# A gated cross-attention and routed-expert layer on one core: the order of four instruction queues between attention and the expert blocks

## The reference

```python
x = x + tanh(g_xattn) * xattn(layernorm(x), ctx)     # 4 x 256 tokens of 256, 64 context rows, 16 heads of 128
h = layernorm(x)                                      # 1024 tokens
combine = top-2 of softmax(h @ gate_w.T), 4 experts   # weight per token and expert, others zero
y = sum_e combine[:, e] * swiglu(h, w1[e], w3[e], w2[e]) + swiglu(h, sw1, sw3, sw2)
x = x + tanh(g_ffn) * y
```

## Time and profile before

| | us |
|---|---|
| median of three runs | 271.18 (270.52 to 271.84) |
| profiled execution | 273.08 |
| its span, first to last instruction | 271.3 |
| TensorE busy | 227.8 (84%) |
| VectorE / GpSimd / ScalarE busy | 148.1 / 131.2 / 119.1 |
| mean granted TensorE clock | 0.957 |

### The profile page before, as it was taken

The page is one execution under the profiler, slowest core; times in us unless marked ns, Lnnn a source line. Parts: engine busy times, 40 slices in busy tenths (PEclk is TensorE's granted clock), DMA queues, the critical chain, the costliest instruction groups (busy, mean ns, idle before and its releaser), DMA issues.

```text
span 271.3 us, 4800 instructions
## 1 busy us (share of the span) xinstructions
PE 227.8 (84%) x1490; PEld 194.0 (72%) x1490; DVE 148.1 (55%) x352; ACT 119.1 (44%) x225; POOL 131.2 (48%) x121
## 2 busy tenths in 40 slices
PE   3999999989969769757776688989999999998920
PEld 1786777879968659646565567878988889887820
DVE  1399889998848556455636417663433435333210
ACT  3376787386543543454423323334344433433310
POOL 4134311748958567844525552164446465452422
PEclk9999999999999995799999959999999999999995
DMA  7753553121413412420002310032423424332131
GB/s 214 228 150 143 164 185 120 58 58 58 138 24 113 138 33 103 135 80 19 19 22 67 108 54 7 0 60 41 77 39 45 75 41 59 58 50 30 23 39 21
DMA packets 12775, 20.99 MB, mean 77 GB/s; under 512 B 2032, under 2 KB 7664, under 8 KB 12752
## 3 DMA queue, kind: packets, MB, share of 16 engines
q1 hardware_dynamic: 9104, 15.71, 18.4%
q0 software_dynamic: 3648, 4.98, 11.5%
HBM read 16.10 MB, written 4.59 MB: 76 GB/s over the span
## 4 chain that ended last, share of the span: by engine, by line
PE 41%; DMA 23%; issue 10%; ACT 8%; POOL 7%; DVE 7%; POOLq 1%; DVEq 1%; SPq 1%; ACTq 0%
DMA out_dram<-probs,tok 19%; PE bankR L358 5%; PE bankQ L242 4%; PE bankQ L244 4%; PE bankQ L243 4%; PE bankP L242 4%; PE bankP L243 4%; PE bankP L244 4%; POOL reg L1411 3%; DMA raw<-kvq_dram 3%; ACT reg L762 2%; ACT probs L805 2%; POOL rstd L1400 2%; PE bankP L335 2%; DMA probs<-x2d,tok 1%
## 5 line engine op out<-in xcount | busy, mean ns | idle before, releaser
L1438 POOL DMA_INDIRECT out_dram<-probs,tok x19 | 30.1, 1587 | 53.3 <-ACT probs L805 30.6
L1411 POOL TENSOR_TENSOR reg<-raw,reg 128x768 fp32r<-128x768 f32 x16 | 29.3, 1833 | 16.5 <-ACT reg L762 16.5
L242 PE MATMUL bankS<-reg,hT 128*128 x76 | 22.9, 301 | 2.4 <-DVE hT L1200 1.5
L1429 POOL DMA_INDIRECT probs<-x2d,tok x19 | 20.2, 1065 | 5.6 <-issue 5.1
L1379 POOL TENSOR_TENSOR w_lo<-raw,w_hi 128x512 fp32r<-128x512 f32 x8 | 10.4, 1301 | 24.4 <-ACT w_hi L686 24.4
L244 PE MATMUL bankS<-reg,hT 128*128 x76 | 21.4, 281 | 0.0
L243 PE MATMUL bankS<-reg,hT 128*128 x76 | 21.4, 281 | 0.0
L1005 DVE TENSOR_TENSOR PT_lo<-bankR,PT_hi 128x512 fp32r<-128x512 f32 x16 | 10.8, 680 | 18.3 <-ACT PT_hi L734 18.3
L792 ACT CAST hT<-bankR 128x512 fp32r<-128x512 f32 x19 | 11.1, 586 | 20.5 <-PE bankR L550 20.5
L1200 DVE TENSOR_TENSOR hT<-bankR,hT 128x512 fp32r<-128x512 f32 x19 | 13.1, 691 | 10.1 <-ACT hT L792 10.1
L1392 POOL TENSOR_TENSOR probs<-probs,rcp 128x1024 f32<-128x1024 f32 x8 | 15.3, 1910 | 4.3 <-DVE rcp L989 4.3
(11 more groups left out here) (232 smaller groups left out, 727.2 us busy)
## 6 DMA issues: line engine op xcount, KB each, us to landing
raw<-ffn_dram SPq DMA_DIRECT2D x18, 384.0 KB, 3.6
raw<-kvq_dram SPq DMA_DIRECT2D x7, 384.0 KB, 3.3
probs<-wo_dram SPq DMA_DIRECT2D x8, 256.0 KB, 2.7
x_sb<-x_dram SPq DMA_DIRECT2D x1, 1024.0 KB, 6.0
x2d<-xn SPq DMA_DIRECT2D x8, 128.0 KB, 1.7
out_dram<-x_sb SPq DMA_DIRECT2D x8, 128.0 KB, 1.7
probs<-x2d,tok POOLq DMA_INDIRECT x19, 2.9
out_dram<-probs,tok POOLq DMA_INDIRECT x19, 3.8
```

The costliest lines, as they stand in the source:

```text
L242: eng.matmul(acc, l_hi, r_hi, start=start, stop=False, **kw)
L1411: pool.tensor_tensor(lo, raw[:, (m + 2) % RS, :], hi.bitcast(F32), ALU.subtract).then_inc(wf_lo, 1)
L1429: pool.indirect_dma_start(out=x_blk[:, i % 4, :], out_offset=None, in_=x2d[:, :], in_offset=bass.IndirectOffsetOnAxis(ap=tok[:, i:i + 1], ...
L1438: pool.indirect_dma_start(out=out[:, :], out_offset=bass.IndirectOffsetOnAxis(ap=tok[:, i:i + 1], axis=0), in_=y_blk[:, i % 4, :], in_offs ...
```

## The change

No computation is added or removed; queues are put in another order, with two waits moved and two added.

- GpSimd subtracts weight tiles two behind the tiles that ScalarE rounds in the same iteration.
- VectorE reads the logits ahead of its part of `split_p`, and chooses the experts of group 0 ahead of the fifth tile's logits; the block list comes earlier, `spots`, the token copies and `settle(1)` are placed anew.
- TensorE makes the first shared up product ahead of the last half of attention; `turn_x2(7)` and the logits come later.
- ScalarE evicts the shared tile n-3 ahead of the activation of tile n.
- The last shared down product and its eviction stand inside block 0.
- GpSimd gathers block n-3 ahead of the addition of shared tile n, and the first gather waits for the first four stored tiles only.

```diff
@@ TensorE
                 wait(pe, h_gate, i - 1)
+                if i == 0:
+                    pe.wait_ge(s_gate, NT)
...
             places(0)
+            pe.wait_ge(wf_lo, JS)
+            pe.wait_ge(x1_ok, NT - 2)
+            shared_up(0)
             attend(7, 1)
             turn_x2(6)
-            pe.wait_ge(wf_lo, JS)
             pe.wait_ge(x1_ok, NT - 1)
-            shared_up(0)
-            gate_logits(6)
             shared_up(1)
             shared_turn(0)
-            turn_x2(7)
+            gate_logits(6)
             shared_up(2)
             shared_turn(1)
+            turn_x2(7)
             pe.wait_ge(settled, 1)
             shared_down(0)
+            shared_up(3)
             gate_logits(7)
-            shared_up(3)
...
             places(1)
+            e = [expert_of(0)]
+            shared_turn(7)
             turn_block(0)
-            shared_turn(7)
             shared_down(6)
-            e = [expert_of(0)]
-            shared_down(7)
             pe.wait_ge(wf_lo, NM)
-            pe.wait_ge(s_out, NT)
             for i in range(NBLK):
                 if i + 1 < NBLK:
                     turn_block(i + 1)
                 up_block(i, e[i])
+                if i == 0:
+                    shared_down(7)
+                    pe.wait_ge(s_out, NT)
@@ ScalarE
             normal_x2(5)
+            split_p(7, 0)
             split_w(15)
-            split_p(7, 0)
             split_p(7, 1)
-            split_x2(5)
-            split_w(16)
-            normal_x2(6)
             act.wait_ge(lsub_ok, 1)
...
+            split_x2(5)
+            normal_x2(6)
+            shared_silu(0)
+            split_w(16)
             split_x2(6)
-            shared_silu(0)
+            shared_silu(1)
             normal_x2(7)
...
             for n in range(3, NT):
+                shared_out(n - 3)
                 shared_silu(n)
-                shared_out(n - 3)
                 shared_split(n - 1)
             shared_out(NT - 3)
+            shared_split(NT - 1)
             split_block(0)
-            shared_split(NT - 1)
             shared_out(NT - 2)
-            shared_out(NT - 1)
...
                 silu_block(i)
+                if i == 0:
+                    shared_out(NT - 1)
@@ VectorE
                 reciprocal(n + 2)
+                read_logits(n - 2)
                 split_p(n + 1, 0)
-                read_logits(n - 2)
...
             split_p(7, 0)
+            choose(0)
             read_logits(4)
-            choose(0)
             split_p(7, 1)
-            split_x2(5)
             add_attention(6)
             statistics(6)
             aggregate(6)
+            split_x2(5)
+            settle(0)
+            shared_gate(0)
             read_logits(5)
-            settle(0)
-            spots(0, 0, 2)
-            split_x2(6)
             add_attention(7)
             statistics(7)
             aggregate(7)
-            shared_gate(0)
+            list_first()
+            split_x2(6)
+            spots(0, 0, 2)
...
@@ GpSimd
-                if i == 0:
+                if i in (0, FIRST):
                     for s in range(2):
-                        pool.wait_ge(x2_st[s], 64)
+                        pool.wait_ge(x2_st[s], 32 if i == 0 else 64)
...
             for n in range(2, 6):
-                split_w(2 * n + 2)
+                split_w(2 * n)
                 scale_x2(n - 1)
-                split_w(2 * n + 3)
+                split_w(2 * n + 1)
                 normal_p(n + 2)
...
             for n in range(3, NT):
+                gather(n - 3)
                 add_shared(n)
-            gather(4)
```

More of the change, by code:

```diff
@@ L877, in _ @@
             act.activation(warm[:, :], mhalf[:, 0:1], ACT.Silu)
+            split_x2(5)
+            normal_x2(6)
+            shared_silu(0)
+            split_w(16)
             split_x2(6)
-            shared_silu(0)
+            shared_silu(1)
             normal_x2(7)
-            shared_silu(1)
+            shared_split(0)
+            shared_silu(2)
+            split_x2(7)
+            shared_split(1)
             split_w(17)
[L884 to L887, removed]
             for n in range(3, NT):
+                shared_out(n - 3)
                 shared_silu(n)
-                shared_out(n - 3)
                 shared_split(n - 1)
             shared_out(NT - 3)
+            shared_split(NT - 1)
             split_block(0)
-            shared_split(NT - 1)
             shared_out(NT - 2)
-            shared_out(NT - 1)
             c = [column_of(0)]
@@ L1313, in _ @@
             aggregate(7)
-            shared_gate(0)
+            list_first()
+            split_x2(6)
+            spots(0, 0, 2)
+            shared_gate(1)
+            shared_split(0)
             read_logits(6)
             spots(0, 2, 4)
-            shared_gate(1)
-            shared_split(0)
+            shared_gate(2)
+            shared_split(1)
             split_x2(7)
             select(0)
-            shared_gate(2)
-            shared_split(1)
+            shared_gate(3)
             read_logits(7)
-            list_first()
-            shared_gate(3)
             shared_split(2)
+            shared_gate(4)
+            shared_split(3)
             read_tokens(0)
@@ L1329, in _ @@
             tokens_of(1)
-            shared_gate(4)
-            shared_split(3)
+            shared_gate(5)
+            shared_split(4)
             tokens_of(2)
             tokens_of(3)
-            shared_gate(5)
-            shared_split(4)
+            shared_gate(6)
+            shared_split(5)
             tokens_of(4)
             choose(1)
-            shared_gate(6)
-            shared_split(5)
-            settle(1)
             shared_gate(7)
             shared_split(6)
+            settle(1)
+            shared_split(7)
+            split_block(0)
             spots(1, 4, 6)
-            split_block(0)
-            shared_split(7)
             for i in range(NBLK):
@@ L1464, in _ @@
             normal_p(1)
+            normal_p(2)
             split_w(2)
-            normal_p(2)
+            scale_x2(0)
+            normal_p(3)
             split_w(3)
[L1469 to L1472, removed]
             for n in range(2, 6):
-                split_w(2 * n + 2)
+                split_w(2 * n)
                 scale_x2(n - 1)
-                split_w(2 * n + 3)
+                split_w(2 * n + 1)
                 normal_p(n + 2)
+            split_w(12)
+            scale_x2(5)
+            split_w(13)
             split_w(14)
-            scale_x2(5)
+            scale_x2(6)
             split_w(15)
-            scale_x2(6)
+            scale_x2(7)
             split_w(16)
-            scale_x2(7)
             split_w(17)
[L1485 to L1489, removed]
+            for n in range(3):
+                add_shared(n)
             for n in range(3, NT):
+                gather(n - 3)
                 add_shared(n)
-            gather(4)
             raise_e(1)
```

## The result

The changed kernel takes 258.29 us (median of 4 runs, 256.24 to 259.74) against 271.51 us (270.52 to 273.41) before: ratio 0.950, 95% interval 0.941 to 0.959. The forecast was 253.6 with 249.5 to 259.5. A second measurement gave 258.12 us, 0.944 (0.937 to 0.951). Of the ten executions in the two measurements, the four with a mean granted clock of 0.970 or more took 255.2 to 257.2 us, the six at 0.953 to 0.960 took 257.4 to 259.7. The profiled execution after took 259.74 us, span 258.0; against its 273.08 the saving is 13.3 us where the prediction's sum has 17.7.

What follows compares the result with a forecast made beforehand. No engine was full before 175.10 us, engines handing one token round; then TensorE. Savings 6.9 + 3.5 + 3.0 + 7.8, less 1.3 and 2.2, gave 17.7 off 273.08: 255.4, scaled 253.6; range 249.5 to 259.5.

Steps and rivals of the forecast that it cites:

- The clean walk: Rival: neither the choice held up by subtractions nor a new clock fall happens; 21.2 us saved, 250.1; chance 0.20.
- No effect: Rival: the gain is taken back at the last scatters; chance 0.04.
- Slower: Rival: the clock does not recover; five blocks at half clock end at 278 us; chance 0.04.
- kept pace: Rival: in the shared expert only 3.5 of 7.8 us go, VectorE being waited for; 13.4 saved, 257.9; chance 0.22.
- Part 4: Shared expert, second half: earlier evictions end waits before down products, last down product moves out; 13.7 us, saved 7.8.
- Part 1: Score loop: weights subtracted two tiles late, logits read earlier; three iterations at TensorE's 7.82 us, saved 6.9.
- the sign: Score loop: under 1 us of ScalarE idle time ahead of the normalisations, with iterations of 7.8 us.
- Part 2: End of attention: GpSimd's chain sets 17.3 us, saved 3.5 against 20.84, before two costs of 1.3 and 2.2.
- (a): End of attention: GpSimd's subtractions hold up VectorE's comparison of the choice; taken at 1.3 us, bounds nothing to 1.8.
- (b): End of attention: one clock fall to 0.50 behind TensorE's idle 4.5 us; taken at 2.2 us, at most 3.4.
- Part 3: Shared expert, first half: reordering covers waits for normalised tiles, 1.0 us idle kept for the block list; 12.85 us, saved 3.0.
- Part 5: First blocks: moved down product and its eviction's wait offset by less low clock and idle time; sum 0.1, taken as nothing.

Runs made afterwards that it cites:

- the filled gap: Changed kernel with 36 extra products, whose result is not read, in TensorE's idle gap ahead of the eighth attention tile: 256.1 us, 0.937.
- The three single remedies: Changed kernel with, one at a time, 36 unread products in TensorE's gap (256.1 us), GpSimd's last five subtractions held back (256.01), block list later (256.12).

## Why the prediction was right, and where it was not

**The forecast** holds in direction and range; its value is 4.7 us low. The rivals fell as follows. The clean walk did not happen: both costs were real. "No effect" is out, since the door moved and the last scatters moved with it (252.55 after, 265.62 in the earlier trace rows). "Slower" is out: every fall ended ahead of the steady stretch, which ran at 1.00. The "kept pace" has the right total (257.9) for a wrong reason, see Part 4.

**Part 1, right.** Iterations of 7.62 to 7.66 us, TensorE busy throughout. GpSimd's 16.5 us ahead of its subtractions became 5.6, ScalarE's 26.7 us ahead of the normalisations 11.4. ScalarE still idles 1.53, 1.03 and 0 us ahead of the loop's normalisations, where the sign said under 1, and TensorE does not wait for it. The loads, priced at nothing, cost nothing: no wait for them shows in the loop. The 0.5 us beyond the forecast are TensorE's own busy time, 7.64 an iteration against the 7.82 taken.

**Part 2, right within 0.8 us and in both costs.** (a) was taken at 1.3: `gt` grew from 0.21 to 1.79, so 1.6. The Trainium skill, SBUF — State Buffer, section "Who interferes with whom", has the later operation fully blocked; these rows agree, 1.79 us for an operation of 0.21. (b), taken at 2.2, is about what the filled gap gives back, some 2 us (258.1 to 256.1). The gap was forecast at 4.5 us and is 4.91. But in the first profile half of the low clock, 3.8 of 7.5 us, lies behind the cut, in Part 3.

**Part 3 failed, and with it 4.2 of the 5.1 us.** The step reads "Of the idle 4.07 us I keep 1.0, for the block list ... 12.85 us; saved 3.0" (11.81 and 1.0 are 12.81). It priced the idle time and took TensorE's 11.81 us at full clock. Three things were left out that the prediction had in hand for Part 2. The clock fall that begins at the end of attention runs on into this stretch (7.5 us, up to 118.2). The subtraction behind the last scaling holds up the list just as others hold up the choice, so TensorE's wait there is 2.89 us, not 1.0. And behind that wait the clock can fall once more, as it did in one of the two profiles. With the subtractions elsewhere the stretch takes 12.82 us, but that this meets the 12.85 is luck: TensorE's work is 10.95 there and not 11.81, its wait for the list 1.87 and not 1.0. So of the wait's 2.89 us some 1.0 is the meeting with the subtraction, for which the sum had no term, and 0.9 was too little taken for the list itself. Ports, gap and clock are one chain. The three single remedies measured about 2 us each, which the change's own executions at the higher clock also reach; keeping the subtractions off the whole choice and the list gives 4.2 in the median, and of the four only this lies clear of the change.

**Part 4, right to 0.8.** Shared tiles are 2.3 to 2.75 us apart (forecast 2.5), no wait for an eviction ahead of a down product is left, and no wait for gathered rows shows in this stretch. The stretch is 14.55 against 13.7, and stays so when the ports are freed (14.56). TensorE's work is 12.15 us where 12.5 was taken, and its waits for the choice, the last low half and the first block's low half are 0.79, 1.19 and 0.42, 2.4 in all where 1.2 was taken.

**Part 5, mis-sized by 1.5.** The wait for the moved eviction was taken at 0.7 and shows as 1.32 us; the credits for less low clock and less idle time did not come, since a fall of 3.4 us (145.50 to 148.90) took the place of the old one. TensorE's work grew by 0.92, the moved product's 0.75 among it. Moving that product ahead saved its wait, but not the time of the kernel. The sign "the first block's up product near 142" missed by the losses of Parts 3 and 4: it stands at 146.07.

## What to carry to other kernels

When a move packs one engine's work, list every short operation of the engine that shares ports with it over the whole stretch, not just the one that the old trace shows blocked: each can cost up to a whole long operation (1.8 us here), and if it stands in front of what TensorE awaits, a fall of the clock can come on top. Follow a predicted stall into the next stretch of the sum. A remedy that only moves the long operation is to be looked up in the next trace, for it will lie beside another step: here `gt`, then `rest`, then `blk` and `nblk`, then `spot`.

## What the runs showed of the hardware

```profile
107.13:110.50 3.37, 3.37 (x18) 3.37 (x18) 1.76 (x5) 1.03 (x4) 3.09 (x5) 0.56 0.20 31
110.50:114.00 3.50, 3.50 (x31) 3.24 (x31) 1.82 (x7) 1.39 (x3) 3.50 (x3) 1.00 0.33 124
```

```profile
106.78:110.00 3.22, 3.22 (x18) 3.22 (x18) 1.76 (x5) 0.88 (x4) 2.94 (x5) 0.59 0.18 29
110.00:115.00 5.00, 5.00 (x28) 4.42 (x29) 1.77 (x6) 1.55 (x3) 4.00 (x3) 0.58 0.25 90
```
